# Projection to q, k and v: the subtraction that makes the third parts of q and k stands on GpSimd instead of VectorE

## The chip, the cores and the metric

One core of one Trainium2 chip. The time is device microseconds (us) of one execution of the whole kernel on that core. The kernel is a chain of phases with a barrier of all engines between two of them. This document is about the phase that projects to q, k and v, which runs from 204 us to 289 us of a span of 1902.7 us.

## The reference

The model is a macaron block on x of shape (4, 1024, 256) in float32. The part that matters here is the attention of its second sub-layer:

```python
x = x + 0.5 * ffn(layernorm(x))             # gated recurrence over the 4 batch rows, then tanh
qkv = jnp.einsum('btc,fc->btf', layernorm(x), w_qkv)
...
scores = jnp.einsum('bhqd,bhkd->bhqk', q, k) * hs ** (-0.5)
```

There are 16 heads of 16 columns. q and k are kept as a sum of three bfloat16 parts each, so that the scores come out in float32 quality from bfloat16 matmuls. Part 0 is the rounded value, part 1 the rounded remainder, and part 2 the remainder less part 1.

## The kernel before, in words

The 4096 tokens are worked on in 8 steps of 512 tokens (a step is `step(n, i, h, left)` in the code; n counts from 0 to 7, h is n modulo 2, `left` is how many steps follow, at most 3). Each engine has its own copy of the step, and semaphores join them; nothing else sets the order. `steps` (L885) runs n = 0 to 3 in a hardware loop and n = 4 to 7 written out.

In a step, TensorE makes four units of 128 rows by 512 tokens (two of q, two of k; L901) in four PSUM banks, then v; after unit 0 it also transposes the normalized x of step n + 1. Each unit u goes through this chain:

- ScalarE `first` (L926) rounds the PSUM bank to part 0.
- VectorE `remainder` (L967) writes PSUM less part 0 to `rest[u % 2]`, a buffer of two slots. It waits until the third part of unit u - 2 has been made, and for u = 0 until all thirds of the step before have.
- ScalarE `second` (L922) rounds the remainder to part 1.
- `third` (L962 before) subtracts part 1 from the remainder and writes part 2.
- SyncE `store` (L1017) writes the three parts to DRAM.

Between these the engines prepare later steps. In the code's order, with the steps' numbers:

- VectorE in step n: the end of the feed-forward for n + 2 (`dve_residual`, L208), its statistics (L127, L130, L135), remainder 0, the low part of the transposed x (`dve_lo`, L169), remainders 1 to 3 with thirds 0 and 1 between them, the sum before the tanh for n + 3 (`dve_add`, L196), thirds 2 and 3.
- ScalarE in step n: first 0, the high part of the transposed x (L165), first 1, second 0, first 2, second 1, first 3, the normalization for n + 2 (`act_apply`, L120), seconds 2 and 3, the tanh for n + 3 (`act_tanh`, L202), the copies of v (L947).
- GpSimd in step n: only three small instructions of the norm for n + 2 (`pool_shift`, L103, L112, L115).

So the tanh of step n feeds the residual of step n + 1. Parts that fall away near the end of the phase: the sum and the tanh run in steps 0 to 4, the residual, the statistics, the shift and the normalization in steps 0 to 5.

Of the kernel before, what the change touches and what calls it, by code (L numbers as in the profile page):

```python
# [11 lines left out]
ALU = mybir.AluOpType  # L12
# [10 lines left out]
GROUPS = TILES // GT  # L23
# [27 lines left out]
class Phase(ExitStack):  # L51
# [7 lines left out]
    def sem(self, name):  # L59
        self.semaphores.append(self.nc.alloc_semaphore(name=name))  # L60
        return self.semaphores[-1]
# [799 lines left out]
def qkv_phase(nc, tag, X, ident, ps, W, V, parts_dram, tail, stacks, loaded):  # L861
# [3 lines left out]
    HALVES = T // GN  # L865
    QK = 2 * KC
    SCALE = (HD ** -0.5, HD ** -0.5, 1.0, 1.0)
    with Phase(nc) as ctx:
        sb = lambda n, s, d: ctx.enter_context(nc.sbuf_tensor(f"{tag}_{n}", s, d))
        sem = lambda n: ctx.sem(f"{tag}_{n}")  # L870
        norm = Norm(nc, lambda n, s, d: ctx.enter_context(nc.sbuf_tensor(n, s, d)),
                    lambda n: ctx.sem(n), ps[:, 0:2], ident, tag)
        part = sb("part", [P, HALVES, QK, PARTS, GN], BF16)
        rest = sb("rest", [P, 2, GN], F32)
        ring = ps[:, 2:2 + RING]
        unit_done, v_done, v_read = sem("unit_done"), sem("v_done"), sem("v_read")
        part0_done, part1_done, part2_done = sem("part0_done"), sem("part1_done"), sem("part2_done")
# [7 lines left out]
        def steps(eng, step):  # L885

            with eng.Fori(0, B - 2) as i:
                step(i * 2, i, 0, 3)
                step(i * 2 + 1, i, 1, 3)
            for left in (3, 2, 1, 0):  # L890
                n = GROUPS - 1 - left
                step(n, n // 2, n % 2, left)

        @block.tensor
        def _(pe):
            def step(n, i, h, left):
                norm.pe_ready(pe, n)
                for u in range(QK):
                    pe.wait_ge(rest_done, n * QK + u + 1)
                    w = lambda p: lambda k: p[:, k, u * P:(u + 1) * P]  # L900
                    matmul3(pe, ring[:, u], w(wh), w(wl), lambda k: norm.xh[:, h, k, :],  # L901
                            lambda k: norm.xl[:, h, k, :], range(KC)).then_inc(unit_done, 1)
                    if u == 0 and left:
                        norm.pe_turn(pe, n + 1, 1 - h)
                for u in range(2):
                    pe.wait_ge(v_read, 2 * n + u + 1)
                    for t in range(2):
                        j = 2 * u + t
                        ins = matmul3(pe, ps[:, 6 + u, t * C:(t + 1) * C],
                                      lambda k: norm.xh[:, h, k, j * P:(j + 1) * P],  # L910
                                      lambda k: norm.xl[:, h, k, j * P:(j + 1) * P],
                                      lambda k: wh[:, k, 2 * C:3 * C], lambda k: wl[:, k, 2 * C:3 * C], range(KC))
                    ins.then_inc(v_done, 1)

            norm.pe_first_turn(pe, norm.var_done, ring[:, 0, 0:P], 6, 5)
            steps(pe, step)
# [40 lines left out]

        @block.vector
        def _(dve):
            def third(n, h, u):  # L960
                dve.wait_ge(part1_done, n * QK + u + 1)
                dve.tensor_tensor(part[:, h, u, 2], rest[:, u % 2], part[:, h, u, 1], ALU.subtract).then_inc(part2_done, 1)  # L962

            def remainder(n, h, u):
                dve.wait_ge(part0_done, n * QK + u + 1)
                dve.wait_ge(part2_done, 1 + n * QK + max(0, u - 1))
                dve.scalar_tensor_tensor(out=rest[:, u % 2], in0=ring[:, u], scalar=SCALE[u],  # L967
                                         in1=part[:, h, u, 0], op0=ALU.mult, op1=ALU.subtract).then_inc(rest_done, 1)

            def step(n, i, h, left):  # L970
                if left >= 2:
                    tail.dve_residual(dve, n + 2)
                    dve.drain()
                    norm.dve_stats(dve, n + 2, h, lambda j: tile_of(n + 2, j))
                remainder(n, h, 0)
                if left:
                    norm.dve_lo(dve, n + 1, 1 - h)
                for u in range(1, QK):
                    remainder(n, h, u)
                    if u < QK - 1:  # L980
                        third(n, h, u - 1)
                if left >= 3:
                    tail.dve_add(dve, n + 3, 1 - h)
                for u in range(QK - 2, QK):
                    third(n, h, u)

            dve.sem_inc(rest_done, RING)
            dve.sem_inc(part2_done, 1)
            for h in range(HALVES):
                dve.sem_inc(stored[h], 16)  # L990
            tail.dve_add(dve, 0, 0)
            tail.dve_add(dve, 1, 1)
            tail.dve_residual(dve, 0)
            dve.wait_ge(tail.x_done, 1)
            norm.dve_stats(dve, 0, 0, lambda j: tile_of(0, j))
            tail.dve_residual(dve, 1)
            norm.dve_apply(dve, 0, 0, lambda j: tile_of(0, j))
            dve.wait_ge(tail.x_done, 2)
            norm.dve_stats(dve, 1, 1, lambda j: tile_of(1, j))
            tail.dve_add(dve, 2, 0)  # L1000
            norm.dve_lo(dve, 0, 0)
            dve.wait_ge(norm.shift_done, 1)
            steps(dve, step)

        @block.gpsimd
        def _(pool):
            norm.pool_setup(pool)
            norm.pool_shift(pool, 0, 0)
            norm.pool_shift(pool, 1, 1)
            with pool.Fori(0, GROUPS // 2 - 1) as i:  # L1010
                for h in range(HALVES):
                    norm.pool_shift(pool, i * 2 + 2 + h, h)

        @block.sync
        def _(sp):
# [1121 lines left out]
```

## Time and profile before

| | |
|---|---|
| Median of 3 runs | 1907.27 us (1904.51 to 1907.8) |
| Profiled execution, its own time | 1904.48 us |
| Profiled execution, span of its instructions | 1902.7 us |
| Busy share over the span: TensorE, VectorE, ScalarE, GpSimd | 91%, 70%, 59%, 48% |
| The same from 236 to 259 us, in the phase changed | 88%, 96%, 84%, 13% |

How to read it: the busy share over the whole span mixes phases that have different limits. The second row of shares belongs to the phase that is changed, in which VectorE is the busiest engine. A high share shows that an engine has much to do; whether it also sets the pace is seen from what each of its instructions waits for.

### The profile page before, as it was taken

To read this page: it belongs to the slowest core of one execution; us is meant where nothing else is said; L and a number is where in the kernel's file an instruction comes from. 1 tells how busy PE (TensorE), PEld (TensorE's weight loads), DVE (VectorE), ACT (ScalarE), POOL (GpSimd) and SP (SyncE) were. 2 spreads that over 40 slices of the span, in tenths; PEclk is the share of its full clock that TensorE was granted. 3 is DMA by queue.
4 is the path that set the end of the run, shared out by engine and by line. 5 is a ranking of instruction groups with operands and counts; after the bars stand their busy time and mean duration, and the time that the engine had idled before them with its cause. 6 is when DMAs were issued, how large, how long until landed. Compare 5 with 4: busy or idle time off the path is not lost. (4 is left out here: it accounts for less than half of the span.)

```text
span 1902.7 us, 30415 instructions
## 1 busy us (share of the span) xinstructions
PE 1727.0 (91%) x9624; PEld 1137.6 (60%) x9624; DVE 1329.4 (70%) x2865; ACT 1122.8 (59%) x1608; POOL 903.9 (48%) x658
## 2 busy tenths in 40 slices
PE   6999897999999999997999799996998999989998
PEld 5887672222222222227888677775666766767776
DVE  4554985777777777775555588875677777768886
ACT  3332688999999999993332222215777777621220
POOL 0001108999999999994004322212545454521111
PEclk9999898999999999998999899998999999999999
DMA  4000275435435335300001000002222233200000
GB/s 154 1 0 12 79 215 87 63 45 78 55 45 85 47 53 76 48 1 12 1 1 34 29 1 0 0 1 69 90 90 89 89 97 103 101 1 23 22 22 22
DMA packets 57642, 96.99 MB, mean 51 GB/s; under 512 B 7936, under 2 KB 29664, under 8 KB 57568
## 3 DMA queue, kind: packets, MB, share of 16 engines
q1 hardware_dynamic: 55392, 94.50, 22.6%
q10 hardware_dynamic: 2176, 1.55, 0.3%
q8 instruction: 41, 0.67, 0.2%
q14 instruction: 33, 0.27, 0.1%
HBM read 78.98 MB, written 17.04 MB: 50 GB/s over the span
## 5 line engine op out<-in xcount | busy, mean ns | idle before, releaser
L1269 POOL TENSOR_TENSOR att_weights<-att_weights 128x1024 f32<-128x1024 f32 x288 | 541.5, 1895 | 16.7 <-DVE att_weights L1213 6.1
L1213 DVE SCALAR_TENSOR_TENSOR att_weights<-att_weights,ps 128x512 f32<-128x512 f32 x576 | 369.8, 683 | 152.1 <-ACT att_weights L1189 150.2
L1189 ACT ACTIVATE att_weights<-att_weights 128x1024 f32<-128x1024 f32 x288 | 302.5, 1051 | 0.0
L1185 ACT ACTIVATE att_weights<-ps 128x1024 f32<-128x1024 f32 x288 | 294.4, 1023 | 9.4 <-PE ps L1131 5.5
L757 DVE SCALAR_TENSOR_TENSOR X<-ps,moe_gsel,X 128x256 f32 (+1 forms) x512 | 246.4, 483 | 64.6 <-PE ps L47 48.7
L1145 PE MATMUL ps<-att_weights,att_v_ones 128*32 128x512 f32 (+3 forms) x1536 | 288.9, 497 | 2.6 <-POOL att_weights L1269 2.5
L47 PE MATMUL ps<-w_experts_hi,moe_xh 128*128 128x512 f32 x512 | 205.2, 401 | 0.0
L47 PE MATMUL ps<-w_experts_hi,moe_xl 128*128 128x512 f32 x512 | 203.1, 397 | 0.0
L47 PE MATMUL ps<-w_experts_lo,moe_xh 128*128 128x512 f32 x512 | 201.6, 394 | 0.0
L1128 PE MATMUL ps<-q_stack,k_stack 128*128 128x512 bf16 (+3 forms) x384 | 117.1, 342 | 29.5 <-DVE att_weights L1213 19.8
L817 POOL TENSOR_TENSOR X<-X,moe_bias_sb 128x512 f32 (+1 forms) x32 | 41.3, 1292 | 208.0 <-DVE X L757 206.7
L330 ACT ACTIVATE ffn_gates<-ps,ffn_gate_bias 128x512 f32<-128x512 f32 x72 | 49.7, 690 | 151.9 <-PE ps L47 145.4
L1128 PE MATMUL ps<-att_q_stack,att_k_stack 128*128 128x512 bf16 (+3 forms) x384 | 114.3, 332 | 22.2 <-DVE att_weights L1213 17.2
L1128 PEld LDWEIGHTS ps<-q_stack,k_stack 128*128 128x128 bf16 x384 | 37.4, 98 | 154.8 <-DVE att_weights L1213 142.7
L1128 PEld LDWEIGHTS ps<-att_q_stack,att_k_stack 128*128 128x128 bf16 x384 | 37.0, 96 | 149.0 <-DVE att_weights L1213 141.9
L103 POOL TENSOR_TENSOR ffn_rstd<-ffn_var,ffn_power 128x4 f32<-128x4 f32 x16 | 16.2, 1013 | 231.2 <-DVE ffn_var L135 231.2
L47 PEld LDWEIGHTS ps<-w_experts_hi,moe_xh 128*128 128x128 f32 x512 | 96.0, 188 | 26.7 <-DVE X L757 3.2
L1145 PEld LDWEIGHTS ps<-att_weights,att_v_ones 128*32 128x32 f32 x1536 | 56.9, 108 | 90.0 <-issue 54.2
L47 PEld LDWEIGHTS ps<-w_experts_lo,moe_xh 128*128 128x128 f32 x512 | 96.1, 188 | 22.3
L47 PEld LDWEIGHTS ps<-w_experts_hi,moe_xl 128*128 128x128 f32 x512 | 96.1, 188 | 20.5
L666 ACT ACTIVATE moe_gT<-ps 96x512 fp32r<-96x512 f32 x16 | 9.5, 595 | 160.0 <-PE ps L597 160.0
L1904 POOL TENSOR_TENSOR ssm_rise<-ssm_rise,ssm_cT 128x512 f32<-128x512 f32 x64 | 94.8, 1506 | 18.8 <-DMA ssm_rise<-decays 18.8
(262 smaller groups left out, 3819.5 us busy)
## 6 DMA issues: line engine op xcount, KB each, us to landing
ssm_lb<-decays SPq DMA_DIRECT2D x32, 512.0 KB, 4.6
ssm_rise<-decays SPq DMA_DIRECT2D x32, 512.0 KB, 3.8
qk_parts<-qkv_part SPq DMA_DIRECT2D x32, 384.0 KB, 2.6
q_stack<-qk_parts SPq DMA_DIRECT2D x64, 128.0 KB, 4.7
k_stack<-qk_parts SPq DMA_DIRECT2D x64, 128.0 KB, 8.2
att_q_stack<-qk_parts SPq DMA_DIRECT2D x64, 128.0 KB, 4.9
att_k_stack<-qk_parts SPq DMA_DIRECT2D x64, 128.0 KB, 8.7
out<-X SPq DMA_DIRECT2D x8, 512.0 KB, 2.9
```

What stands on the lines that cost most here:

```text
L47: ins = pe.matmul(out, l(k), r(k), start=first and n == 0, stop=last and n == len(passes) - 1)
L103: pool.tensor_tensor(self.rstd[:, s], self.var[:, s], self.power[:, :], ALU.pow).then_inc(self.rstd_done, 1)
L330: act.activation(gates[:, m, gate], ring[:, u % RING], ACT.Tanh if gate == 2 else ACT.Sigmoid, bias=bias[:, gate * KC + m:gate * KC + m + ...
L757: dve.scalar_tensor_tensor(out=x, in0=ring[:, e // 2, (e % 2) * C:(e % 2 + 1) * C], scalar=gsel[:, s, j, e:e + 1], in1=x, op0=ALU.mult, op ...
L817: pool.tensor_tensor(x, x, bias_sb[:, pair], ALU.add).then_inc(added, 1)
L1128: ins = pe.matmul(scores(u)[:, t, c:c + w], SK[s][:, h, kj * P:(kj + 1) * P], SQ[s][:, h, q:q + w], start=True, stop=not diagonal)
L1145: ins = pe.matmul(O(qb)[h * 2 * HD:(h + 1) * 2 * HD, q0:q0 + w], va[:, s, kj, h], Wt[:, u % WU, t, c:c + w], start=kj == 0, stop=m in BLOC ...
L1185: act.activation(Wt[:, u % WU], scores(u), ACT.Exp).then_inc(exp_done, 1)
L1189: act.activation(Wt[:, u % WU], Wt[:, u % WU], ACT.Ln, bias=1.0).then_inc(ln_done, 1)
L1213: dve.scalar_tensor_tensor(out=wt[:, t], in0=wt[:, t], scalar=LIMIT, in1=scores(u)[:, t], op0=ALU.min, op1=ALU.max).then_inc(max_done, 1)
L1269: pool.tensor_tensor(Wt[:, u % WU], Wt[:, u % WU], Wt[:, u % WU], ALU.mult).then_inc(sq_pool, 1)
L1904: ins = pool.tensor_tensor(heads, heads, cT[:, v, b].unsqueeze(1).broadcast_to([P, NH // 2, P]), ALU.mult)
```

## The change

The subtraction `third` is taken out of VectorE's program and put into GpSimd's, with the same operands, the same wait (part 1 is done) and the same signal (`part2_done`). GpSimd's program now walks through all 8 steps: first the shift for n + 2, where there is one, then the four thirds. No other engine's instructions change.

```diff
         @block.vector
         def _(dve):
-            def third(n, h, u):
-                dve.wait_ge(part1_done, n * QK + u + 1)
-                dve.tensor_tensor(part[:, h, u, 2], rest[:, u % 2], part[:, h, u, 1], ALU.subtract).then_inc(part2_done, 1)
-
...
                 for u in range(1, QK):
                     remainder(n, h, u)
-                    if u < QK - 1:
-                        third(n, h, u - 1)
                 if left >= 3:
                     tail.dve_add(dve, n + 3, 1 - h)
-                for u in range(QK - 2, QK):
-                    third(n, h, u)
...
         @block.gpsimd
         def _(pool):
             norm.pool_setup(pool)
+            def third(n, h, u):
+                pool.wait_ge(part1_done, n * QK + u + 1)
+                pool.tensor_tensor(part[:, h, u, 2], rest[:, u % 2], part[:, h, u, 1], ALU.subtract).then_inc(part2_done, 1)
+
+            def step(n, i, h, left):
+                if left >= 2:
+                    norm.pool_shift(pool, n + 2, h)
+                for u in range(QK):
+                    third(n, h, u)
+
             norm.pool_shift(pool, 0, 0)
             norm.pool_shift(pool, 1, 1)
-            with pool.Fori(0, GROUPS // 2 - 1) as i:
-                for h in range(HALVES):
-                    norm.pool_shift(pool, i * 2 + 2 + h, h)
+            steps(pool, step)
```

VectorE, step 4 of the phase (the first that is written out), from the statistics to the last instruction of the step. L967 and L963 are the remainder before and after the change, L962 the third, L169 `dve_lo`, L196 `dve_add`.

```order
 L135 TENSOR_SCALAR qkv_var<-qkv_mv 128x4
-L967 SCALAR_TENSOR_TENSOR qkv_rest<-ps,qkv_part 128x512
+L963 SCALAR_TENSOR_TENSOR qkv_rest<-ps,qkv_part 128x512
 L169 TENSOR_TENSOR qkv_xl<-ps,qkv_xh 128x1024
-L967 SCALAR_TENSOR_TENSOR qkv_rest<-ps,qkv_part 128x512
-L962 TENSOR_TENSOR qkv_part<-qkv_rest,qkv_part 128x512
-L967 SCALAR_TENSOR_TENSOR qkv_rest<-ps,qkv_part 128x512
-L962 TENSOR_TENSOR qkv_part<-qkv_rest,qkv_part 128x512
-L967 SCALAR_TENSOR_TENSOR qkv_rest<-ps,qkv_part 128x512
+L963 SCALAR_TENSOR_TENSOR qkv_rest<-ps,qkv_part 128x512 x3
 L196 TENSOR_TENSOR v<-v,ffn_hc 128x1024
-L962 TENSOR_TENSOR qkv_part<-qkv_rest,qkv_part 128x512 x2
```

The four thirds are gone; remainders 1 to 3 and the sum stand directly behind one another.

GpSimd, from the last shift of the loop before to the start of the attention phase (L1257):

```order
L103 TENSOR_TENSOR qkv_rstd<-qkv_var,qkv_power 128x4
L112 TENSOR_SCALAR qkv_shift<-qkv_mv 128x4
L115 TENSOR_TENSOR qkv_shift<-qkv_shift,qkv_rstd 128x4
L1010 REGISTER_ALU
L1010 COMPARE_AND_BRANCH
L64 UNCONDITIONAL_BRANCH
L66 ISA
L1255 UNCONDITIONAL_BRANCH
L1257 MEMSET att_v_ones 128x2048
```

And GpSimd after the change, from the end of the loop (steps 0 to 3) to the end of the phase:

```order
L887 COMPARE_AND_BRANCH
L103 TENSOR_TENSOR qkv_rstd<-qkv_var,qkv_power 128x4
L112 TENSOR_SCALAR qkv_shift<-qkv_mv 128x4
L115 TENSOR_TENSOR qkv_shift<-qkv_shift,qkv_rstd 128x4
L1002 TENSOR_TENSOR qkv_part<-qkv_rest,qkv_part 128x512 x4
L103 TENSOR_TENSOR qkv_rstd<-qkv_var,qkv_power 128x4
L112 TENSOR_SCALAR qkv_shift<-qkv_mv 128x4
L115 TENSOR_TENSOR qkv_shift<-qkv_shift,qkv_rstd 128x4
L1002 TENSOR_TENSOR qkv_part<-qkv_rest,qkv_part 128x512 x12
L64 UNCONDITIONAL_BRANCH
```

L1002 is the third in its new place. Steps 4 and 5 have a shift and four thirds each, steps 6 and 7 thirds alone, so 12 of them stand in a row.

## Rows read from the trace of the kernel before

**Rows 1.** One stretch: length, busy PE, PEld, DVE, ACT, POOL, clock, DMA, GB/s.
```profile
236.00:259.00 23.00, 20.24 (x121) 17.32 (x122) 22.05 (x42) 19.21 (x35) 2.90 (x6) 1.00 0.89 246
```
**Rows 2.** Timeline of VectorE, step 4: start us, us, what, [idle before].
```profile
248.97 1.23 DVE L208 SCALAR_TENSOR_TENSOR X<-v,X 128x1024 f32<-128x1024 f32 x1
...
252.26 0.69 DVE L967 SCALAR_TENSOR_TENSOR qkv_rest<-ps,qkv_part 128x512 f32<-128x512 f32 x1
...
254.00 0.68 DVE L967 SCALAR_TENSOR_TENSOR qkv_rest<-ps,qkv_part 128x512 f32<-128x512 f32 x1
...
257.38 1.21 DVE L196 TENSOR_TENSOR v<-v,ffn_hc 128x1024 f32<-128x1024 f32 x1
258.52 1.28 DVE L962 TENSOR_TENSOR qkv_part<-qkv_rest,qkv_part 128x512 bf16<-128x512 f32 x2
259.82 1.23 DVE L208 SCALAR_TENSOR_TENSOR X<-v,X 128x1024 f32<-128x1024 f32 x1
```
**Rows 3.** Timeline of ScalarE, step 4.
```profile
252.99 0.63 ACT L922 ACTIVATE qkv_part<-qkv_rest 128x512 bf16<-128x512 f32 x1 [1.19 <-DVE qkv_rest L967]
...
254.71 0.63 ACT L922 ACTIVATE qkv_part<-qkv_rest 128x512 bf16<-128x512 f32 x1 [0.61 <-DVE qkv_rest L967]
...
255.73 2.06 ACT L120 ACTIVATE qkv_xn<-X,qkv_shift,qkv_rstd 128x256 f32<-128x256 f32 x4
257.69 1.14 ACT L922 ACTIVATE qkv_part<-qkv_rest 128x512 bf16<-128x512 f32 x2
258.74 1.04 ACT L202 ACTIVATE v<-v 128x1024 f32<-128x1024 f32 x1
```
**Rows 4.** Waits of the phase, one of the longest: total us, times, longest us.
```profile
ACT qkv_part L922 <- DVE qkv_rest L967: 11.3, 14, 1.4
```
**Rows 5.** Timeline of GpSimd, step 4: the end of the shift.
```profile
253.91 0.20 POOL L115 TENSOR_TENSOR qkv_shift<-qkv_shift,qkv_rstd 128x4 f32<-128x4 f32 x1 [0.23 <-POOL qkv_shift L112]
```
**Rows 6.** Timeline, tanh of step 2 and residual of step 3, in the loop.
```profile
236.85 1.05 ACT L202 ACTIVATE v<-v  x1
238.02 1.22 DVE L208 SCALAR_TENSOR_TENSOR X<-v,X  x1
```
**Rows 7.** One line's instructions on GpSimd: count, min/median/max ns, first and last start.
```profile
L457 POOL TENSOR_TENSOR w_qkv_lo<-ffn_raw,w_qkv_hi x3: 1290/1297/1604, 147.5 to 153.0; 128x512 fp32r<-128x512 f32 x3
L1904 POOL TENSOR_TENSOR ssm_rise<-ssm_rise,ssm_cT x64: 1257/1285/2290, 1325.7 to 1666.7; 128x512 f32<-128x512 f32 x64
L1912 POOL TENSOR_TENSOR ssm_xd<-ssm_xdt,ssm_edge x32: 1038/1046/1060, 1337.0 to 1667.9; 128x512 f32<-128x512 f32 x32
```
**Rows 8.** Timeline of GpSimd and VectorE in the feed-forward phase at 1032 to 1036 us.
```profile
1031.89 1.29 POOL L457 TENSOR_TENSOR w_experts_lo<-ffn_raw,w_experts_hi 128x512 fp32r<-128x512 f32 x1
1031.95 1.22 DVE L169 TENSOR_TENSOR ffn_xl<-ps,ffn_xh 128x1024 fp32r<-128x1024 f32 x1 [5.30 <-ACT ffn_xh L165]
...
1033.82 1.29 POOL L457 TENSOR_TENSOR w_experts_lo<-ffn_raw,w_experts_hi 128x512 fp32r<-128x512 f32 x1
1033.83 1.82 DVE L368 TENSOR_TENSOR ffn_gates<-ffn_gates 128x512 f32<-128x512 f32 x1 [0.66 <-ACT ffn_gates L330]
1035.58 0.68 DVE L369 TENSOR_TENSOR ffn_gates<-ffn_gates,ffn_c 128x512 f32<-128x512 f32 x1
```
**Rows 9.** Timeline of GpSimd and VectorE in the state-space phase at 1631 us.
```profile
1631.04 3.52 POOL L1904 TENSOR_TENSOR ssm_rise<-ssm_rise,ssm_cT 128x512 f32<-128x512 f32 x2
1632.04 1.35 DVE L1802 TENSOR_TENSOR ssm_dec<-ssm_dec,ssm_cb 128x1024 f32<-128x1024 f32 x1 [2.78 <-ACT ssm_dec L1670]
```
**Rows 10.** Timeline of ScalarE and VectorE, step 7 to the start of the attention phase.
```profile
280.15 0.62 ACT L922 ACTIVATE qkv_part<-qkv_rest 128x512 bf16<-128x512 f32 x1
...
281.55 0.62 ACT L922 ACTIVATE qkv_part<-qkv_rest 128x512 bf16<-128x512 f32 x1
...
283.69 1.48 DVE L962 TENSOR_TENSOR qkv_part<-qkv_rest,qkv_part 128x512 bf16<-128x512 f32 x2
...
289.25 1.28 ACT L1177 ACT_TABLE_LOAD   x1 [3.39 <-PEq L67]
```

## The prediction

> **What bounds the phase now.** I read the busy times of a stretch first. From 236 to 259 us VectorE is busy 22.05 of 23 us, TensorE 20.24, ScalarE 19.21, GpSimd 2.90 [rows 1]. The obvious reading is that VectorE sets the pace and GpSimd has room. The timelines of VectorE and ScalarE, read side by side over one step, show something else: a circle between the two in which no third stands. It starts with the residual of step 4 at 248.97 on VectorE. Statistics follow it, and remainder 0 starts at 252.26, 3.29 us later; remainder 1 starts at 254.00, 1.74 later, with `dve_lo` between [rows 2]. It ends at 254.68, and ScalarE, which has stood idle for 0.61 us, starts second 1 at 254.71. Then come first 3, the normalization at 255.73, seconds 2 and 3 at 257.69 and the tanh at 258.74, which ends at 259.78 [rows 3]. The next residual needs that tanh and starts at 259.82 [rows 2]. The sum is 3.29 + 1.74 + 0.71 + 1.02 + 1.96 + 1.05 + 1.04 + 0.04 = 10.85 us, exactly the distance of the two residuals. The list of waits says the same: ScalarE waits 11.3 us in all for remainders [rows 4]. The last two thirds of the step run at 258.52 for 1.28 us, to 259.80 [rows 2]. So two things end together: the circle at 259.78 and VectorE's own queue at 259.80. The same holds in the loop, where the tanh ends at 237.90 and the residual starts at 238.02 [rows 6]. Taking the thirds away frees one of two equal limits.
>
> **What is removed.** Four thirds a step, about 0.64 us each in a back-to-back pair [rows 2], some 2.6 us of VectorE a step or 20 us over 8 steps. The gain is only what the residual can start earlier, at most 0.02 us in step 5 and some 0.1 us in the looped steps, where a little of the 0.12 us after the tanh may be VectorE's own bookkeeping [rows 2, 3, 6]. Over five steps that is 0 to 0.4 us; I take 0. The cover of the removed work is the circle through ScalarE.
>
> **What is added on GpSimd.** No row shows a subtraction with a bfloat16 input there. Nearest is the same subtraction at the same size with a narrower output type, 1.29 us; below it lies a product with a repeated second operand, 1.05 us; as upper bound I take 1.5 us, above the usual 1.285 of the product of two full operands, whose maximum of 2.29 is a blocked one, as shown below [rows 7]. I take 1.29. The four of a step are 5.2 us on an engine that is idle for nearly 9, so its throughput is no limit. What counts is who waits for each.
>
> - Thirds 0 and 1. GpSimd comes from its shift at 254.11 [rows 5]. Third 0 runs from 254.15 to 255.44, third 1 from 255.40 (second 1 ends at 255.34) to 256.69. Remainder 3 waits for third 1 and starts at 256.72, and the sum for the tanh 0.61 later, at 257.33 against 257.38 before [rows 2, 3]. It ends at 258.54. The tanh may start at 258.74, so the margin is 0.2 us. This is the wait that replaces the own order of VectorE, and it costs nothing at 1.29; above 1.49 it delays the tanh.
> - Third 2 is ready when second 2 ends, 258.32. The sum L196 runs until 258.54 and reads two tensors of SBUF, which decides the rest.
>
> **Two readers of SBUF.** The trace shows what GpSimd and VectorE do to each other. With one operand in PSUM, VectorE's L169 keeps its 1.22 us beside a subtraction on GpSimd [rows 8]. With both operands in SBUF, L368 starts 0.01 us behind GpSimd's subtraction and takes 1.82 us where its like takes 0.68: it ends 1.83 after GpSimd's start, which is 0.68 of its own after 1.15 of standing. In the second place L1802 ends 2.35 us after GpSimd's start, 1.22 of its own after 1.13, and the second of the GpSimd pair then ends 1.17 us behind it, at 1634.56 instead of about 1633.6 [rows 9]. So one stands until the other has done nearly all of its reading. The remainders (PSUM and SBUF), `dve_lo` and the statistics don't take part; the sum L196 and the residual L208 do, with 1.21 and 1.23 us [rows 2].
>
> So third 2 ends 1.17 after the sum, at 259.71, and third 3, which is ready since 258.83, starts at 259.67. The residual is ready at 259.80 [rows 2, 3]. Third 3 is ahead by 0.13 us and holds the residual: it would end at 259.67 + 1.14 + 1.23 = 262.04 instead of 261.05, so 0.99 late. The residual lies on the circle, and the cost is paid in full each time. In step 0 third 2 is not held up by the sum, and the delay there is some 0.1 less. The pattern keeps its shape from step to step, since the sum, the thirds and the tanh hang on the same chain. It occurs where thirds stand ahead of a residual, at the starts of steps 1 to 5: five times, 4.8 us.
>
> The Trainium skill, page "SBUF — State Buffer", section "Who interferes with whom", has this as a rule: a VectorE instruction with two SBUF inputs contends with a GpSimd instruction that reads SBUF, and whichever issues first keeps the shared read port while the other waits. By that rule the trace agrees, with 1.82 for 0.68 us. By it the sum would be the same 4.8 us if third 3 issues first, and nothing if the residual does.
>
> **The end of the phase.** Remainder 0 of a step now waits for third 3 of the step before. In steps 1 to 5 that one, over at about 260.96, is 3 us ahead of a remainder 0 that follows the late residual by 3.3 us. Into step 6, which has no residual before it, remainder 0 has to wait for two thirds of 1.29 us instead of a pair of 1.28 on VectorE [rows 2], at most 1.3 us more. This shrinks to nothing by step 7, where TensorE gives the pace: seconds 0 and 1 start 1.40 us apart, at 280.15 and 281.55, with nothing of VectorE's between them to fill it [rows 10]. In step 7 third 0 runs 280.8 to 282.1, third 1 to 283.5, remainder 3 to 284.2, second 3 to 284.85, third 3 to 286.15, where the last third of before ends at 285.17 [rows 10]. The last store and the barrier behind it start that much later: +1.0 us on the 289.25 at which the attention begins (0.7 with thirds of 1.05 us, 1.6 with 1.5).
>
> **Sum.** 4.8 + 1.0 = +5.8 us on the profiled execution's 1904.48, which gives 1910.3. The median of the three runs is 2.8 us above that execution, so against the median it is 1913.1.
>
> **Rivals.**
>
> - The residual is ahead of third 3. The lead is only 0.13 us of a reckoning that strings ten durations together; at 1.36 us a third it is gone, since two thirds lie on the way to it. Then VectorE isn't held, third 3 ends later unnoticed, and only the end of the phase costs: +0.6 to +1.0, 1908.1. For it speaks the narrow lead, against it the row in which a GpSimd instruction with a lead of 0.01 us won [rows 8]. Chance 0.22.
> - Another price of the third, with part of the loss. At 1.05 us third 3 starts at 259.36 and lets go at 260.26, 0.46 after the residual is due: five times 0.45 and 0.7 at the end, +3, 1910.3. At 1.5 us the sum ends at 258.96, delays the tanh by 0.25, and third 2 still reads when the residual comes: five times 0.4 and 1.6, +3.6, 1910.9. Chance 0.17.
> - Faster: VectorE's queue was the limit and the circle isn't closed, because a wait that I take as binding isn't. Its place is the residual's start; it decides if the tanh is done well before VectorE's queue ends. Then a step would fall to what TensorE needs, 20.24 / 23 of 10.85 or 9.55 us, and six steps would give 7.8 us: 1899.5. The Trainium skill, page "Perfetto Trace Analysis", section "Optimizing Scalar/DVE Operations", says that offloading may make sense when VectorE is saturated, which would be this case, but warns that the shared SBUF port may cancel it. Against it: tanh and thirds end within 0.02 us [rows 2, 3] and ScalarE's idle 0.61 waits for a remainder, not for a third. Chance 0.06.
> - Worse than forecast: TensorE's pause in each step grows from about 1.5 to 2.5 us, or the thirds also meet the sum in a way that I don't see; +9, 1916.3. The granted clock was 1.00 throughout the stretch [rows 1]. Chance 0.07.
>
> **How the numbers follow.** The forecast has 0.48. A measurement of this kernel tells about 0.2%, 3.8 us, from no change. Slower: nearly all of the forecast, the worst case, and a little of the middle one, 0.52. Same: the first rival, most of the second, a little of the forecast, 0.41. Faster 0.07. The range runs from 1905.8, a little below the first rival, to 1915.5, short of the worst. Of this the forecast's own range is 1911.5 to 1914.5.
>
> **What would show it.** Right: the distance of two residuals L208 near 11.9 us instead of 10.85 to 11.05; that instruction at about 2.1 us or more (max) instead of 1.23; GpSimd's L1002 at 1.29, third 2 a bit longer; remainders at 0.69 as before; the start of the attention phase at about 295. VectorE's idle time rises to some 4 us a step, most of it ended by ScalarE's tanh and seconds. Wrong: L208 at 1.23 (the first rival), L1002 away from 1.29 (the second), residuals 9.6 us apart (the third). The prediction falls if third 3 and the residual meet in the other order.

## Result, and the profile after

| | before | after |
|---|---|---|
| Median of 5 runs each, on one chip | 1906.69 us (1904.51 to 1907.8) | 1915.36 us (1912.1 to 1916.32) |
| Ratio, with its 95% interval | 1 | 1.0043 [1.0028, 1.0057] |
| Profiled execution, its own time | 1904.48 us | 1912.1 us |
| Span of its instructions | 1902.7 us | 1910.3 us |
| The phase, between GpSimd's memsets L97 and L1257 | 189.64 to 289.25 us | 188.93 to 294.36 us |

The changed kernel is 8.2 us slower (5.3 to 10.9; the ratio less 1, times 1906.69). Inside the phase its trace shows 105.43 us instead of 99.61, which is +5.82. The rest lies outside the phase. There the eleven traces of this study differ by up to 7 us (span less phase: 1802.6 us in e1, 1809.9 in e5), so a difference of 2 us there can't be put down to the change.

First the same stretch as in [rows 1], after the change.

```profile
236.00:259.00 23.00, 19.45 (x112) 16.34 (x112) 17.07 (x33) 17.51 (x32) 12.03 (x14) 1.00 0.81 220
```

VectorE's busy time went down from 22.05 to 17.07 us and GpSimd's up from 2.90 to 12.03. The engine that seemed full has 6 us to spare, and TensorE and ScalarE have done less as well. What sets the pace is not the load of any one of the four.

VectorE's timeline from the residual of step 4 to the next one answers to [rows 2] (start us, us, what, then in brackets the idle time before and what ended it).

```profile
250.12 1.95 DVE L208 SCALAR_TENSOR_TENSOR X<-v,X 128x1024 f32<-128x1024 f32 x1 [1.31 <-ACT v L202]
...
254.43 0.69 DVE L963 SCALAR_TENSOR_TENSOR qkv_rest<-ps,qkv_part 128x512 f32<-128x512 f32 x1
...
257.41 0.69 DVE L963 SCALAR_TENSOR_TENSOR qkv_rest<-ps,qkv_part 128x512 f32<-128x512 f32 x1 [0.56 <-POOL qkv_part L1002]
258.85 0.69 DVE L963 SCALAR_TENSOR_TENSOR qkv_rest<-ps,qkv_part 128x512 f32<-128x512 f32 x1 [0.75 <-POOL qkv_part L1002]
259.46 1.22 DVE L196 TENSOR_TENSOR v<-v,ffn_hc 128x1024 f32<-128x1024 f32 x1
261.99 1.95 DVE L208 SCALAR_TENSOR_TENSOR X<-v,X 128x1024 f32<-128x1024 f32 x1 [1.31 <-ACT v L202]
```

GpSimd in the same step (its seconds and tanh on ScalarE are the two lines after).

```profile
256.15 1.16 POOL L1002 TENSOR_TENSOR qkv_part<-qkv_rest,qkv_part 128x512 bf16<-128x512 f32 x1
...
260.56 2.30 POOL L1002 TENSOR_TENSOR qkv_part<-qkv_rest,qkv_part 128x512 bf16<-128x512 f32 x2 [1.81 <-ACT qkv_part L922]
```
```profile
259.87 1.14 ACT L922 ACTIVATE qkv_part<-qkv_rest 128x512 bf16<-128x512 f32 x2
260.91 1.04 ACT L202 ACTIVATE v<-v 128x1024 f32<-128x1024 f32 x1
```

The reader is to see four things. The residual takes 1.95 us instead of the 1.23 of [rows 2], although its inputs are there. Thirds 2 and 3 are one record of 2.30 us from 260.56, so third 3 starts about 1.15 later, near 261.7, some 0.3 us ahead of the residual. The residual starts 11.87 us after the one before it, where [rows 2] has 10.85. And all of the 1.02 us lies between the start of the residual and that of remainder 0, 4.31 us instead of 3.29; the other links of the circle are as in the prediction. The hold is 0.72 of it. The other 0.30 is a gap between the aggregates of the statistics (the first line is that of before):

```profile
251.77 0.38 DVE L130 BATCH_NORM_AGGREGATE qkv_mv<-qkv_stats 128x2 f32<-128x6 f32 x4
...
253.63 0.25 DVE L130 BATCH_NORM_AGGREGATE qkv_mv<-qkv_stats 128x2 f32<-128x6 f32 x2
254.07 0.25 DVE L130 BATCH_NORM_AGGREGATE qkv_mv<-qkv_stats 128x2 f32<-128x6 f32 x2 [0.19 <-issue]
```

Before, the four are one record of 0.38 us from 251.77; here they take 0.69, with nothing waited for that the profile shows. This is in step 4, the first that is written out, and not in step 5.

GpSimd's new line over the phase (x count: min/median/max ns, first and last start; then who waited for it, in us and times), and the phase's end on it.

```profile
L1002 POOL TENSOR_TENSOR qkv_part<-qkv_rest,qkv_part x32: 1154/1170/1177, 208.9 to 289.5; 128x512 bf16<-128x512 f32 x32
...
  DVE qkv_rest L963: 15.4, 17
```
```profile
188.93 0.10 POOL L97 MEMSET qkv_power<- 128x4 f32 x1 [35.43 <-POOLq L67]
...
288.14 2.47 POOL L1002 TENSOR_TENSOR qkv_part<-qkv_rest,qkv_part 128x512 bf16<-128x512 f32 x2 [0.23 <-ACT qkv_part L922]
294.36 1.81 POOL L1257 MEMSET att_v_ones<- 128x2048 f32 x1 [3.75 <-POOLq L67]
```

A third costs 1.17 us on GpSimd. The residual's line shows all the holds at once: its looped four and its written out four together run from 1216 to 1953 ns, where [rows 2, 6] have 1.22 and 1.23 us.

```profile
L208 DVE SCALAR_TENSOR_TENSOR X<-v,X x8: 1216/1836/1953, 191.7 to 262.0; 128x1024 f32<-128x1024 f32 x4, - x4
```

The five held ones take 1.87, 1.80, 1.87, 1.95 and 1.95 us, 3.32 us more in all than before. With the 0.30 us of the gap, 2.2 of the 5.82 us are left. Most of that is TensorE's clock late in the phase (stretches as in the first fence; the clock is the last but two; the first line is that of before).

```profile
272.00:274.00 2.00, 2.00 (x11) 1.64 (x10) 1.93 (x3) 1.60 (x5) 0.00 (x0) 1.00 0.63 216
...
272.00:274.00 2.00, 2.00 (x10) 1.81 (x9) 0.00 (x0) 2.00 (x6) 1.87 (x2) 0.50 0.28 94
274.00:276.00 2.00, 2.00 (x8) 1.57 (x7) 1.48 (x2) 1.22 (x3) 0.42 (x1) 0.67 0.82 275
```

The granted clock is at the lower of its two levels (1.2 GHz) in step 6. In the trace of before both stretches have 1.00. What TensorE did ahead of it, before and after:

```profile
268.69 1.09 PE L150 MATMUL ps<-ident,qkv_xn 128*128 128x128 f32 x8 [1.30 <-ACT qkv_xn L120]
...
271.59 1.70 PE L150 MATMUL ps<-ident,qkv_xn 128*128 128x128 f32 x8 [2.02 <-ACT qkv_xn L120]
```

It had stood idle for 2.02 us, waiting for the normalization, and its transposes then take 1.70 us instead of 1.09. The pause there was 1.30 us before. ScalarE's first 0 of step 6 and of step 7, before and then after:

```profile
270.53 0.59 ACT L926 ACTIVATE qkv_part<-ps 128x512 bf16<-128x512 f32 x1
...
278.31 0.60 ACT L926 ACTIVATE qkv_part<-ps 128x512 bf16<-128x512 f32 x1
```
```profile
273.43 0.59 ACT L926 ACTIVATE qkv_part<-ps 128x512 bf16<-128x512 f32 x1
...
282.81 0.60 ACT L926 ACTIVATE qkv_part<-ps 128x512 bf16<-128x512 f32 x1 [0.85 <-PE ps L47]
```

They are 9.38 us apart instead of 7.78: 1.6 us are lost here. From first 0 of step 7 to the attention are 11.55 us, against 10.94: 0.6 more. So the 5.82 us are 3.3 for holds, 1.6 for the clock, 0.3 for the gap and 0.6 in the last step.

### The profile page after: what moved, and what is told of

Same layout as the page of the kernel before. It is cut to its first block and busy times, and to the rows that moved or that the text cites. A ratio compares the mean times of both kernels' runs of the same rounds, so it can differ in the third digit from the quotient of the medians.

```text
span 1910.3 us, 30380 instructions
## 1 busy us (share of the span) xinstructions
PE 1722.2 (90%) x9577; PEld 1139.8 (60%) x9624; DVE 1313.0 (69%) x2833; ACT 1123.1 (59%) x1608; POOL 939.6 (49%) x690
## 3 DMA queue, kind: packets, MB, share of 16 engines
q10 hardware_dynamic: 2176, 1.55, 0.3%
## 5 line engine op out<-in xcount | busy, mean ns | idle before, releaser
L1128 PE MATMUL ps<-q_stack,k_stack 128*128 128x512 bf16 (+3 forms) x361 | 109.9, 341 | 26.9 <-DVE att_weights L1213 23.1
L1128 PE MATMUL ps<-att_q_stack,att_k_stack 128*128 128x512 bf16 (+3 forms) x360 | 106.4, 329 | 24.2 <-DVE att_weights L1213 19.7
L1131 PE MATMUL ps<-ident,neg 128*128 128x128 bf16 x512 | 95.7, 222 | 10.6 <-DVE att_weights L1213 5.4
```

Source lines behind the costliest of these rows:

```text
L1128: ins = pe.matmul(scores(u)[:, t, c:c + w], SK[s][:, h, kj * P:(kj + 1) * P], SQ[s][:, h, q:q + w], start=True, stop=not diagonal)
L1131: ins = pe.matmul(scores(u)[:, t, c:c + P], neg[:, :], ident16[:, :], start=False, stop=True)
```

## Experiments

All of them stand beside runs of the kernel before on their own chip; the median of before was 1906.67 us beside the first four, 1906.62 beside the next four and 1907.29 beside the last. The expectations of the first four count the phase from the first sum L196 (99.19 us before, 105.01 after), the later ones from the memset L97 (99.61 and 105.43). All results below count from the memset.

### e1_late3: third 3 behind the residual

```diff
                 for u in range(QK):
+                    if u == QK - 1 and left >= 3:
+                        pool.wait_ge(tail.x_done, n + 4)
                     third(n, h, u)
```

> The changed kernel, but in steps 0 to 4 GpSimd makes third 3 only after the residual of the next step is done, so that it can't hold it. Measured by the phase, from the first sum L196 to the memset L1257: 99.19 us before, 105.01 with the change. Theory (third 3 holds the residual at the shared SBUF read, five times 0.6 to 0.7 us, and the longer pause of TensorE that comes of it lets its clock fall in step 6, some 1.6 us): L208 back at 1.22, two residuals 10.9 to 11.1 us apart, granted clock 1.00 in step 6, phase 100.0 to 100.8, of which 1 us is the later end; time 1.0 to 2.0 us above the kernel before. Rival (the 15.4 us that VectorE waits for GpSimd before remainders are the cost): those waits are still there, phase 104 or more.

1908.73 us, ratio 1.0011 [1.0002, 1.002]; the phase 100.59 us. GpSimd's thirds 2 and 3 of step 4, then VectorE's residuals at the starts of steps 4 and 5:

```profile
258.47 1.17 POOL L1002 TENSOR_TENSOR qkv_part<-qkv_rest,qkv_part 128x512 bf16<-128x512 f32 x1 [1.80 <-ACT qkv_part L922]
261.20 1.17 POOL L1002 TENSOR_TENSOR qkv_part<-qkv_rest,qkv_part 128x512 bf16<-128x512 f32 x1 [1.56 <-DVE X L208]
```
```profile
248.75 1.23 DVE L208 SCALAR_TENSOR_TENSOR X<-v,X 128x1024 f32<-128x1024 f32 x1 [1.30 <-ACT v L202]
...
259.90 1.23 DVE L208 SCALAR_TENSOR_TENSOR X<-v,X 128x1024 f32<-128x1024 f32 x1 [1.30 <-ACT v L202]
```

With third 3 out of the way by one wait, the residual is back at 1.23 us and most of the loss is gone, with all 32 thirds still on GpSimd. The clock in 272 to 274 us is 1.00 here, after pauses of TensorE of 1.3 to 1.6 us, so the run takes two things away together: the holds (3.32 us) and the fall of the clock. They add up to the 4.84 us between this phase and the one of the changed kernel. What stays, 0.98 us, is the gap between the aggregates, which this trace has too (0.30 us; the distance of these two residuals is 11.15 instead of 10.85), and 0.67 us behind the last residual. The runs e5 and e8 below tell the two apart.

```profile
  DVE qkv_rest L963: 14.9, 17
```

This is the line of who waits for GpSimd's thirds, in this run. VectorE still waits 14.9 us for them before its remainders, nearly the 15.4 of the changed kernel. Yet the distances of its residuals are 11.11, 11.03, 10.95 and 11.15 us, those of before 11.10, 11.03, 10.95 and 10.85: apart from the gap in step 4 they agree to 0.01 us. The holds went, this wait stayed, and the time followed the holds: in these steps the wait is idle time that nobody needs.

### e2_half: thirds 0 and 1 on GpSimd, 2 and 3 on VectorE

The first two lines stand in VectorE's step behind the sum, the others in GpSimd's.

```diff
+                for u in range(QK - 2, QK):
+                    third(n, h, u)
...
-                for u in range(QK):
+                for u in range(QK - 2):
                     third(n, h, u)
```

> Thirds 0 and 1 on GpSimd, thirds 2 and 3 on VectorE behind the sum as before. GpSimd does nothing at the start of the residual, and no third of GpSimd lies at the end of the chain. Theory: L208 at 1.22, distance of residuals 10.85 to 11.1, phase 99.0 to 99.7, time within 1 us of the kernel before. Rival (each third on GpSimd has its price): half of the loss, phase about 102, +3 to +4 us.

1906.97 us, ratio 1.0006 [0.9997, 1.0015]; the phase 100.10 us, 0.49 longer than before. Its residual is unheld:

```profile
259.58 1.23 DVE L208 SCALAR_TENSOR_TENSOR X<-v,X 128x1024 f32<-128x1024 f32 x1
```

Thirds 0 and 1 can be moved at no measurable cost. It is the last two that cost in the steps. The gap between the aggregates isn't in this trace (its residuals are 10.84 us apart), so the 0.49 us are all at the end of the phase.

### e3_no_thirds: no third parts at all

```diff
                 dve.wait_ge(part1_done, n * QK + u + 1)
-                dve.tensor_tensor(part[:, h, u, 2], rest[:, u % 2], part[:, h, u, 1], ALU.subtract).then_inc(part2_done, 1)
+                dve.sem_inc(part2_done, 1)
```

> The kernel before without any third: VectorE only waits for part 1 and signals, part 2 is filled with zeros once at the start, so the third parts of q and k are left out of the result. It measures what the 32 subtractions cost on VectorE. Theory (the circle of residual, remainders, normalization, tanh sets the step): distance of residuals 10.75 to 11.0, phase 98.0 to 99.0, time 0 to 1.5 us less than before. Rival (VectorE's load is the limit, 96% busy): distance 9.4 to 9.6, phase 90 to 92, time 7 to 9 us less.

This kernel leaves the third parts out and sets their places to zero once. 1906.63 us, ratio 1.0004 [0.9995, 1.0013]; the phase 98.89 us, 0.7 shorter. The residuals of steps 4 and 5:

```profile
248.99 1.23 DVE L208 SCALAR_TENSOR_TENSOR X<-v,X 128x1024 f32<-128x1024 f32 x1 [2.13 <-ACT v L202]
...
259.84 1.23 DVE L208 SCALAR_TENSOR_TENSOR X<-v,X 128x1024 f32<-128x1024 f32 x1 [2.13 <-ACT v L202]
```

They are 10.85 us apart, to the hundredth the distance of [rows 2], though VectorE now stands idle for 2.13 us ahead of each, waiting for the tanh. VectorE's 22.05 busy us in 23 had fallen to 15.96 there. So the removed work had a worth of 0 inside a step, as the circle of the prediction has it, and 0.7 us at the end of the phase, where there is no circle any more. This is the run that refutes the rival "faster".

### e4_fill: TensorE's pause filled in each step

```diff
                     if u == 0 and left:
+                        for _ in range(12):
+                            pe.matmul(ps[:, 0, 0:P], ident[:, :], ident[:, :], start=True, stop=True)
                         norm.pe_turn(pe, n + 1, 1 - h)
```

> The changed kernel with 12 idle 128x128 matmuls on TensorE ahead of each transposition, in the pause in which it waits for the normalized x; nothing of their output is used. It takes away the fall of the clock in step 6 alone. Theory: clock 1.00 through step 6, L208 still 1.8 to 1.95, step 6 (first 0 to the next first 0) 7.8 us instead of 9.38, phase 103.2 to 103.8. Rival (the fall is covered by ScalarE and VectorE): step 6 stays at 9.4, phase 105.

1920.05 us, ratio 1.0074 [1.0061, 1.0087]; the phase 111.21 us. As a test of the clock it failed, for the fill was too large:

```profile
228.68 2.84 PE L905 MATMUL ps<-ident 128*128 128x128 f32 x24
```
```profile
236.00:259.00 23.00, 23.00 (x158) 21.03 (x157) 16.70 (x31) 17.93 (x31) 11.01 (x13) 1.00 0.89 227
```

The 12 multiplications are 24 in the record and last 2.84 us, longer than the pause that they were to fill. TensorE is busy 23.00 of 23 us at a clock of 1.00, and it became the limit itself. That says only that TensorE has no 2.84 us to give in a step of 11.9.

### e5_fill_step5: the fill halved, and in step 5 alone

```diff
                     if u == 0 and left:
+                        if left == 2:
+                            for _ in range(6):
+                                pe.matmul(ps[:, 0, 0:P], ident[:, :], ident[:, :], start=True, stop=True)
                         norm.pe_turn(pe, n + 1, 1 - h)
```

> The changed kernel with 6 idle matmuls ahead of the transposition of step 5 alone (1.4 us by the fill of the run before, inside a pause of 2.0 us), so that TensorE isn't late for its own work. Theory: no fall of the clock in step 6, which goes from 9.4 us (first 0 to first 0) to 7.8 or 8.4; phase (memset L97 to memset L1257) 103.7 to 104.5 instead of 105.43, L208 unchanged at 1.8 to 1.95. Rival: the fall of the clock costs nothing, phase 105.3 or more.

1911.88 us, ratio 1.0023 [1.0013, 1.0033]; the phase 103.88 us, 1.55 shorter than that of the changed kernel. The two stretches that had 0.50 and 0.67:

```profile
272.00:274.00 2.00, 1.03 (x9) 1.00 0.83 286
274.00:276.00 2.00, 2.00 (x10) 1.00 0.16 48
```

(These are of TensorE alone: length, its busy time, clock, DMA share, GB/s.) The fill takes away TensorE's pause in step 5 (it runs from 260.47 to 261.97, straight into the transposes); the next pause, in step 6, is 1.71 us instead of 2.02. The clock stays at its upper level there and 1.55 us come back (first 0 of steps 6 and 7 are 7.82 us apart again), while the residuals stay held at 1.87, 1.82, 1.87, 1.94 and 1.96 us. The same trace shows where such a fall costs nothing:

```profile
249.00:251.00 2.00, 1.47 (x9) 0.74 1.03 202
251.00:253.00 2.00, 2.00 (x6) 0.50 1.09 290
```

Here the clock fell in step 4, as in e8, and the residuals on either side are 11.86 us apart against 11.87 in the changed kernel. There the circle leaves TensorE some 2 us of slack in a step. Behind step 5 there is neither residual nor tanh, and ScalarE's firsts wait for TensorE. Whether the shorter pause or the filled one ahead of it kept the clock up, this run doesn't tell.

### e6_early_tanh_dve and e7_early_tanh_pool: the circle opened

The circle is closed by an order: the tanh of a step stands behind seconds 2 and 3, and its sum behind all remainders. Both were moved forward, in e6 in the kernel before (thirds on VectorE), in e7 in the changed one (thirds on GpSimd). The lines with `dve_add` are VectorE's, the others ScalarE's.

```diff
                 for u in range(1, QK):
                     remainder(n, h, u)
+                    if u == 1 and left >= 3:
+                        tail.dve_add(dve, n + 3, 1 - h)
...
-                if left >= 3:
-                    tail.dve_add(dve, n + 3, 1 - h)
...
+                if left >= 3:
+                    tail.act_tanh(act, n + 3)
                 if left >= 2:
                     norm.act_apply(act, n + 2, h, lambda j: tile_of(n + 2, j))
                 for u in range(QK - 2, QK):
                     second(n, h, u)
-                if left >= 3:
-                    tail.act_tanh(act, n + 3)
```

> The kernel before with the sum of step n + 3 moved behind remainder 1 on VectorE and its tanh ahead of the normalization on ScalarE. The thirds stay on VectorE. The circle through the tanh would shorten by 3 us, but VectorE's own queue still holds thirds 2 and 3, which wait for seconds 2 and 3, ahead of the residual. Theory: no gain, steps of 11.3 to 11.7 us, phase 101 to 104, time +2 to +5 us. Rival (VectorE's load alone sets the pace): steps of 10.85, phase 99.6.

> The same reordering on the changed kernel, with the thirds on GpSimd, so that nothing stands between remainder 3 and the residual on VectorE. Theory (the circle was what hid the freed 20 us of VectorE): the step falls to what TensorE or ScalarE needs, 9.4 to 9.9 us, even with a residual or a sum held by a third now and then; phase 92 to 95, time 4.5 to 7.5 us below the kernel before. Rival (holds at the shared read and the remainders' waits for GpSimd eat it): steps of 10.8 or more, phase 99 to 101.

e6: 1910.23 us, ratio 1.002 [1.001, 1.003], the phase 103.82 us. e7: 1903.08 us, ratio 0.9973 [0.9962, 0.9984], the phase 95.75 us. The residuals of e6, then those of e7 in the same part of the phase:

```profile
250.75 1.22 DVE L208 SCALAR_TENSOR_TENSOR X<-v,X 128x1024 f32<-128x1024 f32 x1
...
262.40 1.22 DVE L208 SCALAR_TENSOR_TENSOR X<-v,X 128x1024 f32<-128x1024 f32 x1
```
```profile
236.02 1.22 DVE L208 SCALAR_TENSOR_TENSOR X<-v,X  x1
...
239.22 1.15 DVE L135 TENSOR_SCALAR qkv_var<-qkv_mv 128x4 f32<-128x4 f32 x1
...
242.79 1.46 DVE L196 TENSOR_TENSOR v<-v,ffn_hc 128x1024 f32 x1
...
245.99 1.22 DVE L208 SCALAR_TENSOR_TENSOR X<-v,X 128x1024 f32<-128x1024 f32 x1
```

With the thirds on VectorE the new order is worse: its steps are 11.65 to 11.87 us. With the thirds on GpSimd its steps are 9.93 to 10.05 us, shorter than the 10.85 of before, and this version is faster than both kernels, by 0.27% than before (0.16 to 0.38). So the room that the change makes on VectorE has a worth after all, but only for an order in which the circle doesn't set the step. Neither edit alone gains: the move costs 0.43%, the order 0.2%. The gain stayed below what was expected, though: steps of 9.4 to 9.9 us and 4.5 to 7.5 us in the time were expected, and 3.5 us came. GpSimd in the same part of the phase shows where VectorE waits for it:

```profile
238.05 2.30 POOL L1002 TENSOR_TENSOR qkv_part<-qkv_rest,qkv_part 128x512 bf16<-128x512 f32 x2 [2.74 <-ACT qkv_part L922]
...
243.61 1.66 POOL L1002 TENSOR_TENSOR qkv_part<-qkv_rest,qkv_part 128x512 bf16<-128x512 f32 x1 [0.45 <-ACT qkv_part L922]
```

Third 3 runs until 240.35, and the small L135 and remainder 0 of the next step come behind it. And here VectorE's sum L196, which started at 242.79, holds third 1 in its turn: 1.66 us instead of 1.17, to 245.27. Remainder 3 waits for that one, and the residual stands behind it.

### e8_changed_again: the changed kernel once more

> The changed kernel once more, for a second profile and more times. Theory: phase 105.4 where the clock falls in step 6, some 1 to 1.6 less or more in an execution where it falls in no step or in another one; L208 1.8 to 1.95 in all of steps 1 to 5; time 6 to 9 us above the kernel before.

1914.05 us, ratio 1.0033 [1.0022, 1.0044], the phase 105.41 us. The residuals take 1.87, 1.81, 1.87, 1.95 and 1.95 us, as in the first trace. The clock in step 6 fell again, one stretch later (it fell in step 4 as well, where the residuals stayed 11.88 us apart):

```profile
274.00:276.00 2.00, 2.00 (x6) 1.61 (x5) 0.51 (x1) 1.96 (x5) 1.39 (x2) 0.50 0.34 114
276.00:280.00 4.00, 4.00 (x19) 3.29 (x19) 2.60 (x4) 2.75 (x6) 1.94 (x2) 0.84 0.57 192
```

The loss repeats to 0.02 us in the phase. In this trace the pause ahead of step 5's transposes was 0.80 us, since TensorE was late, and the clock still fell in step 6 behind a pause of 2.02 us.

### e9_var_on_pool: the small instruction that is held in e7

In e7 the variance L135, of 128x4 elements, takes 1.15 us beside GpSimd's thirds instead of the 0.17 that it has in the changed kernel. If this lay on the path, moving it would shorten the step. So GpSimd makes the variance itself, behind its thirds. Shown is GpSimd's step; L135 is taken out of VectorE's program, and epsilon is set once at the start.

```diff
     def pool_shift(self, pool, n, s):
+        pool.wait_ge(self.mv_done, n + 1)
+        pool.tensor_tensor(self.var[:, s], self.mv[:, s, :, 1], self.eps[:, :], ALU.add).then_inc(self.var_done, 1)
         self.pool_rstd(pool, n, s)
```

> The kernel with the early tanh and the thirds on GpSimd, in which the small variance instruction L135 (128x4, epsilon added) stood 0.8 to 1.15 us instead of 0.17, beside third 3 on GpSimd. Here GpSimd adds epsilon itself, so that nothing of VectorE's with that access stands between the statistics and remainder 0. Theory (that instruction is held like the residual was, though it is small): steps of 9.4 to 9.7 us instead of 10.0, phase 93.0 to 94.8 instead of 95.75, time 1 to 3 us lower than with the early tanh alone. Rival (ScalarE's order sets 10.0, the hold is covered): steps and phase as they were.

1903.42 us, ratio 0.9979 [0.997, 0.9989], the phase 97.30 us: no gain over e7, and steps of 10.1 us. GpSimd and VectorE:

```profile
239.12 2.29 POOL L1008 TENSOR_TENSOR qkv_part<-qkv_rest,qkv_part 128x512 bf16<-128x512 f32 x2 [2.73 <-ACT qkv_part L928]
```
```profile
241.51 0.69 DVE L969 SCALAR_TENSOR_TENSOR qkv_rest<-ps,qkv_part 128x512 f32<-128x512 f32 x1 [1.25 <-POOL qkv_part L1008]
```

The idea fell. Remainder 0 waits for third 3 itself, which ends at 241.41; in e7 the held L135 lies inside that wait (thirds until 240.35, remainder 0 at 240.45). Without the hold the wait is bare, 1.25 us, and remainder 0 starts 4.41 us after the residual, where it was 4.43 in e7. Taking away a hold helps only where the next instruction is otherwise ready.

## Why the prediction was right, point by point

**The circle, and that VectorE's queue isn't the limit.** Right. With no thirds at all the step is 10.85 us (e3), and with all thirds on GpSimd and third 3 out of the way the looped steps agree with before to 0.01 us (e1). The busy share of 96% [rows 1] was true and said nothing on the pace.

**Third 3 ahead of the residual.** Right in all five places, and the order was the shaky point. The lead in step 4 was 0.30 us instead of the reckoned 0.13, mostly since a third takes 1.17 us and not 1.29. Putting third 3 behind the residual removed the hold and with it the loss (e1).

**The size of the hold.** Too large in the sum. The prediction had 0.99 each, 4.8 us in all; the rows show 0.58 to 0.72, 3.32 us. The step of it that was off is the price of the third: the shorter third both starts earlier and lets go earlier. In step 4 third 3 starts at about 261.69, and the residual ends at 263.94; its own 1.23 us taken off, it was free to go at 262.71, which is 1.02 us after third 3's start. That is the relation that [rows 9] gave, 1.13 of 1.29, now with a shorter instruction. With a third of 1.17 us the prediction's own sum would have been 1.02 less 0.30, or 0.72, for each. The prediction also let the sum L196 hold third 2 back; in step 4 second 2 ends so late that third 2 starts at 260.56, 0.12 us before the sum is over, and the pair takes 2.30 us, so nothing of this is seen.

Two signs of the prediction have to be read with this. It wanted residuals near 11.9 us apart, and 11.87 was measured in step 4. That is luck: 0.30 of it is the gap, and in the steps of the loop, which have no gap, they are 11.74, 11.61 and 11.59 us apart (before 11.10, 11.03 and 10.95). And L208 was to reach 2.1 us or more, and reached 1.95. The third at 1.17 us also lies halfway to the 1.05 of the second rival, whose sum is a little low: the prediction's own rule for the start of third 3 gives 259.43 there and not 259.36.

The Trainium skill, page "SBUF — State Buffer", section "SBUF: two separate sides", says that of a VectorE instruction with two SBUF inputs and a GpSimd instruction the one that starts first has the shared pair for the whole instruction. That a lead decides, the trace bears out (it was first by 0.30 us in step 4, and held the residual in all five steps); "the whole" it does not quite, since the residual was let go after 1.02 us of an instruction recorded with 1.17.

**The end of the phase, +1.0 us.** Right in kind, a little large: the last step is 0.6 us longer. The prediction had 1.0 with thirds of 1.29 us and 0.7 with 1.05, so for 1.17 its own terms give some 0.85. The last third does end 0.94 us later, counted from first 0 of step 7 (7.80 us instead of 6.86). What was wrong is that the rest starts that much later: the attention follows the last third by 3.75 us and not by 4.08. Why, no run shows. Half of the thirds on GpSimd cost 0.49 there (e2).

**The gap between the aggregates, 0.3 us.** Missed, and no row of before speaks of it. The changed kernel has it in both traces, e1 too, and e2, e3, e6 and the kernel before don't. It goes with VectorE's program, from which all four thirds are gone in the first three (and in e4, e5 and e7, which have the gap too), but not with the thirds alone: in e9 they are gone as well, with L135, and the four aggregates are one record of 0.38 us again. What it is wasn't tried.

**The clock of TensorE.** Missed as a term of the sum. The prediction named a longer pause of TensorE, from 1.5 to 2.5 us, as the worse rival with a chance of 0.07 and gave it +9 us, with no word on a fall of the clock. It came in a smaller size beside the forecast: the pause grew from 1.30 to 2.02 us, the clock fell for under 4 us in step 6, and that cost 1.6 us (1.55 in e5). So 3.3 for holds, 1.6 for the clock, 0.3 for the gap and 0.6 at the end stand where the prediction had 4.8 and 1.0. Both are 5.8 us in the phase, and this agreement is partly luck: an overpriced hold and a missed fall of the clock cancel. The mechanism that carries the largest part is the one named.

**VectorE's new idle time.** 5.9 us of 23, so 3 a step and not 4, and mostly not ended by what was foreseen: GpSimd's thirds end 15.4 us of it in the phase, the tanh 7.2 (the list of waits of the changed kernel from 205 to 290 us: total us, times, longest).

```profile
DVE qkv_rest L963 <- POOL qkv_part L1002: 15.4, 17, 3.4
...
DVE X L208 <- ACT v L202: 7.2, 5, 1.8
```

A remainder waits for third u - 2, and that comes later from GpSimd than from VectorE's own queue. It cost nothing, since remainders 2 and 3 are not on the circle (e1).

**Against the median.** 1915.36 us against a forecast of 1913.1. That is inside the wide range, 0.1 us under its upper end, and outside the forecast's own 1911.5 to 1914.5; it lies nearer to the worse rival's 1916.3 than to the forecast. The repeat gave 1914.05. By the ratios the two are 8.2 and 6.3 us above before. The phase explains 5.8 us, which both intervals hold; the other 0.5 to 2.4 us are outside it.

**What stays open.** Why the clock falls behind some pauses of TensorE and not behind others of the same length; what the gap between the aggregates is; where the time outside the phase goes; and whether the 10.0 us steps of e7 could come down to some 9.5, for which TensorE is busy in them (21.84 of 23 us). For one thing, remainder 0 would have to stop waiting for third 3, and the code has it wait for more than it needs: it writes the slot of `rest` that third 2 read last, while third 3 reads the other one. A wait looser by one third wasn't tried.

## What to carry to other kernels

Follow the instruction that starts each step back through the engines for one full step before moving work off the busiest one: if the walk returns to itself and the busy engine's other work isn't on it, moving that work gains nothing, and emptying the engine altogether is the quickest test. Look at what the moved instruction runs beside in its new place: here a GpSimd instruction of 1.17 us that reads SBUF, 0.3 us ahead of a VectorE instruction with two SBUF operands, delayed it by 0.72 us, and a single wait that put it behind gave that back. Freed room is worth something only with an order that uses it: here the move lost 0.4%, the order lost 0.2%, and the two together gained 0.3%.

## What was not expected of the hardware

- A VectorE instruction of 128x4 elements is held as well. L135, with one operand in SBUF, takes 0.17 us alone and 0.81 to 1.15 us beside GpSimd's thirds (e7). The prediction had left the statistics, to which it belongs, out of this. The Trainium skill, page "SBUF — State Buffer", section "Who interferes with whom", counts its kind among those that can take the shared pair in the two-port modes. The trace agrees in that it is held; which mode it ran in, no run shows.
- A subtraction with a bfloat16 second operand and a bfloat16 result takes GpSimd 1.17 us for 128x512, less than the 1.29 us of the one with float32 operands [rows 7].
- In the changed kernel the holding instruction is not slowed itself: all 32 thirds lie between 1154 and 1177 ns. In e7, where VectorE's sum is under way first, it is the third that is held, for 1.66 us instead of 1.17.
- TensorE's clock fell to its lower level behind a pause of 2.02 us in step 6, in both traces of the changed kernel, and behind none of the pauses of 1.3 to 1.6 us in the traces of before and of e1. Not every pause of 2.02 us does it: in step 5 of the changed kernel one left the clock at 1.00 (first trace), and in step 4 it stayed up in the first trace and fell in the repeat. In e6 it fell behind pauses of 1.87 and 2.09 us and stayed up behind one of 2.30. A fall costs only where somebody waits for TensorE: 1.6 us in step 6, nothing in step 4.
